# Linear attention: the keys of 30 units are transposed by VectorE in 32x32 blocks instead of by TensorE

## What is computed

```python
qkv = silu(hidden_states @ qkv_w.T)               # q, k, v of 32 heads, 64 wide
def step(state, blk):                             # one block of tokens
    qi, ki, vi = blk
    aw = einsum('bhid,bhjd->bhij', qi, ki) * dd
    intra = einsum('bhij,bhjd->bhid', aw, vi)
    inter = einsum('bhid,bhde->bhie', qi * qd_, state)
    new_state = state * bd_ + einsum('bhsd,bhse->bhde', ki * kd_, vi)
    return (new_state, intra + inter)
attn = _rmsnorm(attn, norm_w)
gate = sigmoid(hidden_states @ gate_w.T)
return gate * attn @ out_w.T
```

## Time and profile before

| | |
|---|---|
| Median of three runs | 1079.34 us (1078.82 to 1080.51) |
| Profiled execution, its own time | 1080.03 us |
| Its span | 1078.3 us |
| TensorE matmul busy | 1043.4 us, 97% |
| VectorE busy | 594.3 us, 55% |
| ScalarE busy | 615.7 us, 57% |
| GpSimd busy | 490.6 us, 46% |
| Granted TensorE clock, mean | 0.998 of full speed |
| Linear attention's last L700 | at 619.0 us |

### The profile page before, as it was taken

One profiled execution on the slowest core, in us unless ns is written; L12 is line 12 of the kernel. 1 busy time (PEld: TensorE's weight loads), 2 busy tenths in 40 slices (PEclk: granted clock), 3 DMA queues, 4 the chain that ended last, 5 costly groups with the idle time before them and its releaser, 6 DMA issues. The chain is left out here.

```text
span 1078.3 us, 33515 instructions
## 1 busy us (share of the span) xinstructions
PE 1043.4 (97%) x14381; PEld 822.5 (76%) x14384; DVE 594.3 (55%) x1328; ACT 615.7 (57%) x1169; POOL 490.6 (46%) x527
## 2 busy tenths in 40 slices
PE   5999999999999999999999999988899999999998
PEld 4888889888888988888898888866544444445787
DVE  6243433434343353645545673598877788785543
ACT  4544444444443555555454676776577777767763
POOL 2354454455453564655555454864233332221446
PEclk9999999999999999999999999999999999999999
DMA  3100100101001011102102320057622222300001
GB/s 137 58 3 3 59 2 16 45 2 51 17 2 50 18 31 66 32 25 74 31 18 89 101 70 1 1 134 218 133 53 50 50 48 49 60 3 1 1 20 59
DMA packets 19613, 50.77 MB, mean 47 GB/s; under 512 B 2687, under 2 KB 13759, under 8 KB 16575
## 3 DMA queue, kind: packets, MB, share of 16 engines
q1 hardware_dynamic: 19470, 48.67, 16.2%
HBM read 37.71 MB, written 10.75 MB: 45 GB/s over the span
## 5 line engine op out<-in xcount | busy, mean ns | idle before, releaser
L1915 DVE TENSOR_REDUCE aa_mx<-aa_S 128x1 f32<-128x640 f32 (+1 forms) x192 | 173.4, 952 | 42.4 <-PE aa_S L1626 41.1
L520 DVE SCALAR_TENSOR_TENSOR la_y<-la_g,la_O 128x512 f32<-128x512 f32 x64 | 41.1, 684 | 234.9 <-PE la_O L710 234.3
L1824 ACT ACTIVATE aa_PT<-keep 128x512 f32<-128x512 f32 (+1 forms) x203 | 110.6, 584 | 41.4 <-PE keep L1650 40.0
L1551 POOL TENSOR_SCALAR_AFFINE_SELECT aa_PT<-aa_PT 128x256 f32<-128x256 f32 (+1 forms) x112 | 49.3, 440 | 177.3 <-ACT aa_PT L1824 174.1
L299 POOL TENSOR_TENSOR la_qd<-q,la_C 128x512 f32<-128x512 f32 x64 | 81.1, 1288 | 95.1 <-PE la_O L710 95.1
L312 POOL TENSOR_TENSOR la_yl<-la_y,la_yh 128x512 fp32r<-128x512 f32 x62 | 79.2, 1299 | 87.7 <-ACT la_yh L394 87.7
L320 POOL TENSOR_TENSOR fin_sqacc<-fin_sqacc,la_sq 128x512 f32<-128x512 f32 x64 | 86.1, 1346 | 6.5 <-DVE X L1218 1.9
L509 DVE SCALAR_TENSOR_TENSOR la_S<-la_S,la_C,la_Y 128x64 f32<-128x64 f32 x448 | 88.7, 274 | 0.2
L1096 POOL TENSOR_TENSOR f_fl<-f_f,f_fh 128x512 fp32r<-128x512 f32 x48 | 61.8, 1301 | 58.3 <-ACT f_fh L961 58.2
L1623 PE MATMUL aa_S<-aa_stacks 96*128 96x512 bf16 (+3 forms) x320 | 81.2, 319 | 3.4 <-DVE aa_mx L1915 3.0
L1650 PE MATMUL keep<-aa_stacks 99*128 99x512 bf16 (+3 forms) x259 | 72.2, 327 | 3.9 <-ACT aa_PT L1824 1.5
(11 more groups left out here) (334 smaller groups left out, 3042.2 us busy)
## 6 DMA issues: line engine op xcount, KB each, us to landing
la_Wraw<-w_quads_dram SPq DMA_DIRECT2D x7, 1280.0 KB, 5.7
aa_stacks<-k_parts SPq DMA_DIRECT2D x16, 256.0 KB, 6.5
q_parts<-aa_QP SPq DMA_DIRECT2D x8, 384.0 KB, 4.9
aa_stacks<-q_parts SPq DMA_DIRECT2D x8, 384.0 KB, 4.5
k_parts<-aa_KP SPq DMA_DIRECT2D x8, 384.0 KB, 4.9
qw_w<-w_ffn_dram SPq DMA_DIRECT2D x12, 192.0 KB, 2.4
q_ffn<-qw_w SPq DMA_DIRECT2D x12, 192.0 KB, 1.9
X<-hidden_dram SPq DMA_DIRECT2D x4, 512.0 KB, 7.6
```

Source lines behind the costliest of these rows:

```text
L1824: act.activation(PT[:, (NM2 * g + b) % NPT, h:h + nh, 0:w], ST[at % NB][:, 0:nh * w].rearrange("p (h q) -> p h q", h=nh), ACT.Exp, scale=S ...
L1915: dve.reduce_max(out, src, AXX).then_inc(s1_free, 1)
```

## The change

In the units with keys 1 to 30 TensorE's `turned_keys` is gone; keys 0 (ahead of the loop) and 31 (in the last j = 6) stay there. VectorE has a `turned_keys` of its own: sixteen transposing instructions for a unit, each on 32 partitions and 256 elements (2 pairs x 4 groups x 32), which together write all 4x4 blocks of 32x32 straight from `k` into `kd`, both in SBUF. Instruction number `at` reads the partition quarter `at // 4` and writes the quarter `at % 4`. In unit j VectorE does key j + 2, in three parts: six (with `c`: two) behind the masks, one between the two sums, and nine (with `c`: thirteen) behind `split`. The last one signals kb_ok. Key 1 is done in one go ahead of the loop. ScalarE's `keys` now takes kd as its source and scales it in place. The wait at the head of each set is for k's evictions, and no buffer is added.

```diff
+QUAD, NTURN = 32, 16
...
-            def keys(i, j, pr):
+            def keys(i, j, pr, banks=None):
...
-                    kbv = Y[h][:, pr * GC * LD:(pr + 1) * GC * LD].rearrange("p (c n) -> p c n", c=GC)
+                    kbv = kdv[:, :, h * LD:(h + 1) * LD]
+                    if banks is not None:
+                        kbv = banks[h][:, pr * GC * LD:(pr + 1) * GC * LD].rearrange("p (c n) -> p c n", c=GC)
                     act.activation(kdv[:, :, h * LD:(h + 1) * LD], kbv,
                                    ACT.Copy, scale=C[:, slot, s:s + 1]).then_inc(kd_ok, 1)
...
-                        keys(*step(i, j + 1), pr)
+                        keys(*step(i, j + 1), pr, Y if last and j == 6 else None)
...
-                keys(0, 0, pr)
+                keys(0, 0, pr, Y)
...
+            def turned_keys(i, j, a, b):
+                n, m = step(i, j)
+                if a == 0:
+                    dve.wait_ge(silu_ok, 64 * i + 8 * j)
+                for at in range(a, b):
+                    f, t = slice(at // 4 * QUAD, (at // 4 + 1) * QUAD), slice(at % 4 * QUAD, (at % 4 + 1) * QUAD)
+                    ins = dve.transpose(kd[t].rearrange("p r (c n) -> p r c n", c=GC)[:, :, :, f],
+                                        k[f, m % 2].rearrange("p r (c n) -> p r c n", c=GC)[:, :, :, t])
+                if b == NTURN:
+                    ins.then_inc(kb_ok, 1)
...
+                ahead = has(last, j, 2) and not (last and j == 5)
+                if ahead:
+                    few = 6 if c is None else 2
+                    turned_keys(i, j + 2, 0, few)
...
                     for n in range(2):
                         sums(i, j, n)
+                        if ahead and n == 0:
+                            turned_keys(i, j + 2, few, few + 1)
...
                 if j % 4 < 3 and not (last and j >= 4):
                     split(i, j)
+                if ahead:
+                    turned_keys(i, j + 2, few + 1, NTURN)
...
             masks(0, 1)
+            turned_keys(0, 1, 0, NTURN)
             dve.wait_ge(init_ok, 4)
...
-                if has(last, j, 1):
-                    turned_keys((j + 1) % 8)
+                if last and j == 6:
+                    turned_keys(7)
                 carried(j)
```

## The result

The changed kernel takes 1084.01 us (median of 20 runs, 1081.09 to 1086.26); the kernel before, run beside it, 1080.78 (20 runs, 1078.82 to 1082.91). The ratio is 1.0028, 95% interval 1.0019 to 1.0037: slower by 0.28%, 3.2 us, where I had forecast 4.4 us less. The time lies above the range that I gave, 1060 to 1083.

The account below looks back on a forecast made before the run. TensorE, busy for 97% of the span, was taken to bound the kernel. Removing its transposes gave -19.2 us and new waits in twelve units +14.8, so -4.4 from the 1079.34 us median: 1074.9 us, range 1060 to 1083.

Parts of the forecast that it names:

- One transposition, 0.445 us: On VectorE: each 256-element transposition on 32 partitions takes 0.445 us, not overlapped with the one before.
- Rival 1: On VectorE: transpositions overlap at 0.33 us each, so the run takes 18.9 us less, 1060.4 us; chance 0.22.
- The removal, 0.64 us a unit: On TensorE: dropping sixteen transposes in 30 of 32 units saves 0.64 us each, 19.2 us in all.
- rival 4: On TensorE: the idle gap ahead of the unit widens, taking some 2 us off the gain; no separate chance.
- Six, one, nine hidden in ordinary units; key 1 hidden: On VectorE: these fit into idle time and slack, and key 1's 7.1 us into a 13.9 us wait; no cost.
- Thirteen not hidden: In twelve units with a quantised piece, TensorE waits 1.22, 1.40, 1.60 or 0.73 us ahead of state_sums; 14.8 us together.
- ScalarE's copies: Behind VectorE's transpositions: four SBUF copies of 518 ns each take 1.72 us as a set, 1.8 us with hand-overs.
- The sum: Whole kernel: 19.2 us gained less 14.8 us of new waits, 4.4 us faster, 1074.9 us as median.
- break-even at p = 0.473: Whole kernel: the gain is zero if one transposition takes 0.473 us; within 0.2% between 0.459 and 0.487, chance 0.15.
- 0.72 for faster: Chance that the kernel gets faster: 0.40 for the main case, 0.22 for overlap, 0.10 for the stretch between.
- Rival 3: Thirteen transpositions behind the split last over 0.487 us each; at 0.53, 9.4 us slower, 1088.7 us; chance 0.13.

Follow-up runs that it names:

- halves: The changed kernel with kb_ok signalled behind the 8th and 16th transposition and ScalarE's copies ordered by heads; 1074.30 us, ratio 0.9939 to the kernel before.
- halves3: As halves, with three instead of two transpositions behind the masks in units with a piece of the quantisation; 1070.85 us, ratio 0.9901 to the kernel before.
- before_pad128: The kernel before with 128 always-met waits (64 instructions) at the start of TensorE's program; 1088.01 us, ratio 1.0079 to the kernel before.
- before_pad256: The kernel before with 256 always-met waits (128 instructions) at the start of TensorE's program; 1089.30 us, ratio 1.0076 to the kernel before.
- pad128: The changed kernel with 128 always-met waits (64 instructions) at the start of TensorE's program; 1077.83 us, ratio 0.9978 to the kernel before.
- own_quarter: The changed kernel with each transposition writing the partition quarter it reads (output not the reference's); 1068.45 us, ratio 0.9885 to the kernel before.
- late_hidden: The changed kernel with the four hidden-state loads held back until unit 29's outputs are done; 1079.48 us, ratio 0.9992 to the kernel before.

## Why the prediction was wrong

- **One transposition, 0.445 us.** Right: 0.45. The rule of the Trainium skill ("VectorE: DVE Perf Modes", section "Two Vector instructions with no wait between them"), that an instruction whose output starts in another group of 32 partitions than the last output is held until the earlier ones are done, is borne out: 0.33 to 0.37 from start to start within a quarter, 0.40 to 0.45 across. Rival 1 (0.33) needed the opposite; its price is that of transpositions which stay.
- **The removal, 0.64 us a unit.** Right: 18.93 and 18.81 us a unit became 18.29 and 18.17. The gap of 0.4 us went over to L723, and rival 4, the gap that widens, didn't come.
- **Six, one, nine hidden in ordinary units; key 1 hidden.** Right; no wait for kd in any ordinary unit.
- **Thirteen not hidden.** Right in place, count and size: 1.12, 1.32, 1.58 and 0.64 us for the four kinds of unit against 1.22, 1.40, 1.60 and 0.73, together 13.9 against 14.8 (15.5 by the ledger, with the weight loads). halves and halves3 took the waits away by the amounts that the same arithmetic gives.
- **ScalarE's copies.** 1.70 for 1.72 us as a set; one took 498 ns, not 518.
- **The sum.** This is the step that failed: "The sum is a difference between two spans". It took all that the change does not touch to keep its length, a term put at nothing. At unit 29, with all of the change's own gains and waits in, it was 3.0 us ahead against my 4.4. Behind it 7.4 us were lost, 5.0 of them in gaps where TensorE waits for no semaphore, 0.5 at the passage and 1.7 to the clock that fell behind them. I had counted what every moved instruction does, and not that taking 32 instructions a unit out of TensorE's program (16 matmuls, 16 weight loads) moves all later ones within it, and with them the points at which it runs out of instructions. Another 1.4 us of the 9.1 between 1074.9 and 1084.01 is the base: three runs gave 1079.34 for the kernel before, twenty 1080.78. The break-even at p = 0.473 and the chances were worked out without this, so the range was too narrow above by its size, and the 0.72 for faster too high.
- **Rival 3**, the only one on the slower side, named another mechanism, a transposition above 0.487 us. It did not happen. (Its 17.6 us for sixteen ordinary units at 0.68 us each would be 20 to 24 by the two units shown; nothing else used that.)

**What is shown of the gaps, and what isn't.** Shown: with the VectorE work unchanged they go when TensorE's instructions are shifted (6 us), and without any VectorE transposition they appear by the same shift (7 us); two of them go when loads beside them are moved (3 to 4 us); they stand at the same instructions in different executions. The DMA queues of the changed kernel, 585 to 597 us and 597 to 600 us (queue: packets, MB, share of 16 engines), show one such late transfer:

```profile
q1 hardware_dynamic: 891, 2.16, 58.7%
...
q1 hardware_dynamic: 116, 0.46, 48.3%
q8 instruction: 1, 0.02, 1.8%
```

Twelve microseconds pass without a packet of instructions while data fill 59% of the DMA engines' time, and the gap of 1.98 us ends 2.5 us behind the start of the next one. In the kernel before there are two packets of instructions between 585 and 597 us.

That the packet is TensorE's follows from a count in the traces. I number all that TensorE's queue ran, from the start: matmuls, weight loads, semaphore instructions. The thirteen profiles have 34 gaps of over 0.45 us with "issue" behind 25 us. In every one the instruction that came late has 256 n + 193 or 256 n + 194 records before it; in the changed kernel they are 1985, 20674, 20930, 21441 and 21697. And every one ends 2.2 to 2.7 us behind the start of a packet of 16,384 bytes on q8, the queue of instructions: the five at 73.96, 599.93, 603.68, 615.94 and 622.46 us behind packets that start at 71.26, 597.46, 601.06, 613.58 and 620.12. So TensorE gets its instructions 256 at a time (64 bytes each, if the packet holds just these), and in a gap it has used up one lot before the next is there. That is Theory F. The packet of 597.46 starts when TensorE has four instructions left.

Not shown: why that packet starts so late. Moving loads took this gap away, yet there are gaps of 0.55 to 0.89 us at 38, 74 and 329 us as well, in some executions.

**Like with like.** The change takes 30 x 32 = 960 instructions out of TensorE's program, three and three quarters of 256. With 64 in front, the kernel before is therefore cut into lots as the changed kernel is at the end of the stage, and the gaps of before_pad128 stand at the same instructions, with two, one and fourteen matmuls of their groups left. In the same way before_pad256 lies like pad128 (33 left in both). The first pair gives 1088.01 and 1084.01 us, the change 4.0 us faster; the second about 1083.7 (1089.30 less the late start of 5.6) and 1077.83, 5.9 faster. The forecast was 4.4. The pairs are not alike in everything: the gaps have other lengths (3.1 us in before_pad128, 5.0 in the changed kernel), and before_pad128 loses 1.5 us ahead of the first unit, where the change has moved nothing yet. So this bears out the sign and the rough size of the forecast, and no more.

The kernel before is thus itself a lucky placement, and the verdict on the change depends on it: as it stands 0.28% slower than before; with both programs shifted by the same 64 instructions, 1077.83 against 1088.01, 0.9% faster, and there the lucky placement is the changed kernel's.

## What to carry to other kernels

When work goes from the engine that bounds the kernel to one that has room, compare the new work not with that engine's idle share but with the shortest stretch between its last duty and the first wait behind the moved result; here twelve of thirty units had 0.6 to 1.6 us too little, and a signal at half the work and one instruction moved forward gave it back (1084 to 1071 us). A difference of less than 1% in a long program that is written out may come from where its instructions lie: before judging such a change, look for idle time inside a group of matmuls that no semaphore can explain, count the instructions between two such gaps (here multiples of 256), and run both kernels again with the bounding engine's program shifted by some instructions whose own cost is covered. Choose the shift so that the two are cut alike in the stretch that counts: here 960 fewer instructions, so 64 more.

## What the runs showed of the hardware that I had not expected

- TensorE stood idle for 0.6 to 2.6 us in the middle of groups of matmuls, without any wait in the program, and only at every 256th instruction, 2.2 to 2.7 us behind the start of a 16,384-byte packet on an instruction queue (34 gaps in the thirteen profiles). 128 met waits at the head of its program changed the time of one kernel by -6 us and of the other by +7 us.
- Met waits went two to an instruction, one instruction each 0.106 us: 128 were done at 7.7 us, 256 at 14.6, so they are not cheap once they aren't covered.
- A VectorE transposition of 32x256 started 0.07 us before the end of the one in front when it wrote the same quarter of the partitions, and 0.01 after it when it wrote another (own_quarter).
- A gap can cost more than its length: behind the one at 632.59 us (1.25 us long) the granted clock was 0.50, 1.2 GHz, for 3.4 us, with TensorE busy all the while. It need not: late_hidden has a gap of 1.26 us at the same passage and no fall there. In halves3, with a gap of 2.60 us, it fell three times between 590 and 625 us.
